# One block for the count matrix and the three graph layers, with relation rows fetched by POOL and stored by other engines

## The chip, the cores and the metric

The kernel runs on one core of one Trainium2 chip. The metric is the device time of one execution in microseconds (us); lower is better.

## The reference, cut to what matters

```python
def _L0_gnn_ref(x, edge_index, mask_embed, Wl, Wr, b, gamma, beta, rmean, rvar):
    N, E, D, L = (3125, 100000, 256, 3)
    src, dst = (edge_index[0], edge_index[1])
    h = x.at[0].set(mask_embed)
    deg = jax.ops.segment_sum(jnp.ones((src.shape[0],), h.dtype), dst, num_segments=N)
    deg = jnp.maximum(deg, 1.0)[:, None]
    for i in range(L):
        agg = jax.ops.segment_sum(h[src], dst, num_segments=N) / deg
        z = agg @ Wl[i] + b[i] + h @ Wr[i]
        z = (z - rmean[i]) * jax.lax.rsqrt(rvar[i] + EPS) * gamma[i] + beta[i]
        if i != L - 1:
            z = jax.nn.relu(z)
        z = z + h
        h = z
    return h
...
# in _L1_gnn_ref: a row of a 500-row relation table for every edge
    r_uv = r_hc[edge_type]
    m = clifford_linear(h_src * r_uv, msg_w, msg_b)
    gate = jax.nn.sigmoid(r_uv.reshape(r_uv.shape[0], -1) @ gate_w.T + gate_b)
...
x = x + _L0_gnn_ref(_layernorm(x), edge_index, ...)                # three layers, 103,125 edges
x = x + _L0_ffn_ref(_layernorm(x)[None], ...)[0]                   # 16 experts, top 2
x = x + _L1_gnn_ref(_layernorm(x), edge_index, edge_type_500, ...)  # relation messages
x = x + _L1_ffn_ref(_layernorm(x)[None], ...)[0]                   # 8 experts, top 2
```

Features have 256 columns. The part touched by the change is the first graph network: three times a sum of `h[src]` over the edges of each destination, divided by the degree, two 256 x 256 products, a normalization, relu and a residual. The second graph network needs, for each edge, a row of a table of 500 relations; those rows (260 floats with the gate) are fetched ahead of time, during the stages before it.

## The kernel before, in words

Nodes are held in NT = 25 tiles of 128. Edges are sorted by destination, 103,125 of them in 808 tiles of 128.

**Count matrix.** Since the same sum over edges is needed three times, `build_matrix` (L981) makes an fp8 matrix of 3200 x 3200 that counts the edges between a source and a destination. It works in 196 strips of SW = 16 destinations. A strip has DEEP = 5 tiles of edge records. DVE compares the source's place in its tile with a row of numbers (`b_at`, L1054, three of the five tiles; ACT makes the other two, L1085 and L1090) and writes five one-hot rows of 400 columns for the pair of source tile and destination (`b_oh`, L1058). PE multiplies them, five matmuls of 400 columns into one PSUM bank of a ring of seven (L1071), and ACT writes the bank into the matrix (L1095). Seven strips are a batch, there are 28 batches. For each batch SP reads seven starts from a table (L1026) and issues seven record DMAs (L1033); two batches are in flight (Q = 2). The loops are hardware loops of 14 strips.

**Layers.** `gnn0_layers` (L1113) then runs 3 x 25 destination tiles. h is held as three bf16 parts whose sum is h (256 columns each, with a column of ones for the degree). For each of 25 source tiles PE does one 512-column matmul (`ly_low`, L1181) and one of 256 or 257 (`ly_high`, L1182) with the same weights, a 128 x 128 block of the matrix. Between the sources it places the transposes (L1192) and the product with the two weight matrices (`ly_dense`, L1203) of the tile before. DVE adds the three sums, each divided by the degree, to z, the part of the layer computed ahead (`ly_zin`, L1257 to L1259), applies relu and adds h (L1261, L1264), and splits the next layer's features (L1272 to L1283). ACT copies (L1232, L1234, L1236) and makes one pass over a row block of the matrix for each tile of layers 0 and 1, a row sum (L1239) and the check that no count is above 15 (L1241). SP loads z (L1148) and stores the next layer's z (L1153). h itself stays in SBUF.

**Relation rows.** `RelationRows` (L1354) runs on POOL alone, beside every stage: cast a group of indices (L1375), gather a tile of 128 rows by an indirect DMA (L1383), and store a pair of tiles (L1390) from a ring of four. The 808 tiles are shared among the stages: 32 and 32 in `edge_blocks` (L360) and `gnn0_start` (L854), 160 in the matrix stage (buffer `rr_buf`), 408 in the layers (`rl_buf`), 176 in the first expert stage, by `RelationPairs` (L1618, `f_rr_buf`). A block of the program ends on all engines together.

Of the kernel before, what the change touches and what calls it, by code (L numbers as in the profile page):

```python
# [7 lines left out]
ALU = mybir.AluOpType  # L8
# [3 lines left out]
BF16 = mybir.dt.bfloat16  # L12
# [57 lines left out]
SHARES = (32, 32, 160, 408, 176)  # L70
assert sum(SHARES) == EDGE_TILES
GW = 3 * D + 2
TURN, DENSE = 9, 14
MOST = 15
# [285 lines left out]
def edge_blocks(nc, c, loads, relation):  # L360
# [6 lines left out]
    with Core(nc) as k:  # L367
# [486 lines left out]
def gnn0_start(nc, c, I, x_dram, h_table, room, g, z, folded, relations):  # L854

    with Core(nc) as k:
# [10 lines left out]
        work = RelationRows(nc, c, k, "r0", *relations[1], 2)  # L867
        with nc.Block() as block:
# [94 lines left out]
            def _(sp):  # L963
                sp.wait_ge(s_norm, NT)
                sp.dma_start(h_table.rearrange("(t p) d -> p t d", p=P), h[:, :, :]).then_inc(s_saved, 16)
                sp.wait_ge(s_w, 4)
# [3 lines left out]
                for b in range(NJ):  # L970
                    sp.wait_ge(s_z0, (b + 1) * J)
                    sp.dma_start(z[b * J * P:(b + 1) * J * P, :].rearrange("(t p) d -> p t d", p=P), f.z[:, b * J:(b + 1) * J, :])\
                        .then_inc(s_saved, 16)
                sp.wait_ge(s_saved, 16 * (5 + NJ))

            @block.gpsimd
            def _(pool):
                work(pool)


def build_matrix(nc, c, records, m, relation_work):  # L981

    with Core(nc) as k:
        Q, R, OWN, BANKS = 2, BATCH_S, DEEP - 2, 7
        unroll = Q * R
# [8 lines left out]
        pad = MW - STRIPS * SW  # L998
# [16 lines left out]

        strips = k.ps("b_strips", [P, BANKS, 512])
        s_rec = [k.sem(f"b_rec{q}") for q in range(Q)]
        s_code, s_gap, s_oh, s_at, s_sum, s_m = (k.sem(f"b_{x}") for x in ("code", "gap", "onehot", "at", "sum", "m"))
        rounds = STRIPS // unroll
        with nc.Block() as block:  # L1020

            @block.sync
            def _(sp):
                with sp.Fori(0, rounds) as i:
                    for q in range(Q):
                        starts = [sp.value_load(c.tab["a_start"][0:1, bass.ds(i * unroll + (q * R + n), 1)], min_val=0,  # L1026
                                                max_val=EDGE_TILES * P) for n in range(R)]

                        sp.wait_ge(s_oh, i * unroll + (q + 1) * R)
                        sp.wait_ge(s_at, i * unroll + (q + 1) * R)  # L1030
                        for n in range(R):
# [1379 lines left out]
```

## Time and profile before

| | us |
|---|---|
| median of 3 runs | 3740.11 (3734.98 to 3756.62) |
| profiled execution | 3740.51 |
| its span | 3738.8 |
| busy PE, DVE, ACT, POOL in the span | 2537.3, 1447.2, 1412.6, 2258.4 |

The span is the time from the first to the last instruction of that execution; busy times are averages over stages with different limits, so they are read stage by stage. The matrix stage lies from 272 to 661 us, the layers from 661 to about 1378, the first expert stage lies between 1380 and 2100, and the aggregation over relation edges follows. The granted TensorE clock, averaged over the run, is 0.832 of full speed.

### The profile page before, as it was taken

The page shows a single profiled execution, that of the slowest core. Times are in us where ns is not written, and L with a number is a line of the kernel's source. Part 1 is how long each engine was busy: PE and PEld are TensorE (multiplying, and loading weights), DVE is VectorE, ACT ScalarE, POOL GpSimd, SP SyncE. Part 2 cuts the span into 40 slices and gives each one's busy share as a digit, 9 for nine tenths or more (in the row PEclk, how much of TensorE's full clock was granted, in tenths as well). Part 3 has the DMA queues.
Part 4 walks back from the last instruction along what each step waited for, and adds up shares of the span by engine and source line. Part 5 has one row for each costly group of instructions (what it writes and reads, how often), then busy time and mean ns, then how long its engine had stood idle before and what let it go on. Part 6 is the DMA issues. An engine that isn't in the chain of part 4 may idle for free. (4 is left out here: it accounts for less than half of the span.)

```text
span 3738.8 us, 50034 instructions
## 1 busy us (share of the span) xinstructions
PE 2537.3 (68%) x12155; PEld 1728.3 (46%) x12155; DVE 1447.2 (39%) x4219; ACT 1412.6 (38%) x3615; POOL 2258.4 (60%) x2388
## 2 busy tenths in 40 slices
PE   0155564999999974977404666666666666699990
PEld 0122221555555544776403444444444445588990
DVE  4069997233333224000294444444444445200003
ACT  0037886334432002322105444444444443355550
POOL 0458888777777835777537777777777770111105
PEclk9998999999999985998756767676667667799995
DMA  2554343556666534668427777777777761442213
GB/s 104 185 179 129 115 115 112 177 186 194 193 193 192 184 99 163 194 211 264 150 66 229 207 204 206 200 206 206 205 202 204 201 187 53 148 136 79 81 29 106
DMA packets 320233, 606.95 MB, mean 162 GB/s; under 512 B 83139, under 2 KB 167817, under 8 KB 319239
## 3 DMA queue, kind: packets, MB, share of 16 engines
q0 software_dynamic: 123600, 359.43, 32.1%
q1 hardware_dynamic: 193591, 244.38, 21.1%
q8 instruction: 92, 1.51, 0.2%
q10 hardware_dynamic: 2848, 0.79, 0.1%
q14 instruction: 102, 0.84, 0.1%
HBM read 448.39 MB, written 157.66 MB: 162 GB/s over the span
## 5 line engine op out<-in xcount | busy, mean ns | idle before, releaser
L602 POOL DMA_INDIRECT agg_r_rows<-h_table,b_src x856 | 857.9, 1002 | 321.7 <-issue 217.6
L651 PE MATMUL agg_r_sums<-agg_r_rows,agg_r_onehot 128*128 128x257 f32 x1712 | 701.2, 558 | 380.9 <-DVE agg_r_rows L623 318.2
L651 PEld LDWEIGHTS agg_r_sums<-agg_r_rows,agg_r_onehot 128*128 128x128 f32 x1712 | 429.6, 274 | 636.9 <-issue 572.0
L1181 PE MATMUL ly_low<-parts,matrix 128*128 128x512 bf16 x1875 | 623.3, 380 | 29.1 <-PEq L112 29.1
L623 DVE TENSOR_TENSOR agg_r_rows<-agg_r_rows,agg_r_rel 128x514 f32<-128x514 f32 x428 | 299.0, 699 | 642.6 <-DMA agg_r_rows<-h_table,b_src 640.5
L1182 PE MATMUL ly_high<-parts,matrix 128*128 128x256 bf16 (+1 forms) x1875 | 513.0, 274 | 0.0
L1383 POOL DMA_INDIRECT rl_buf<-r_table,rl_kind x408 | 394.9, 968 | 153.6 <-issue 118.0
L569 ACT ACTIVATE agg_r_gap<-iota,b_near 128x128 f32<-128x128 f32 x856 | 295.0, 392 | 498.8 <-PE agg_r_sums L651 467.4
L1972 POOL DMA_INDIRECT f_xb<-xn_table,f_token x120 | 115.1, 960 | 502.1 <-PE f_pX L1780 363.0
L1790 PE MATMUL f_pH<-f_xT,f_w 128*128 128x128 f32 x2816 | 364.2, 289 | 67.3 <-DMA f_w<-in_L_ffn_w 44.9
L1790 PEld LDWEIGHTS f_pH<-f_xT,f_w 128*128 128x128 f32 x2816 | 349.4, 203 | 98.7 <-DMA f_w<-in_L_ffn_w 49.7
L1955 DVE TENSOR_TENSOR f_yb<-f_pY,f_b 128x256 f32<-128x256 f32 x120 | 50.9, 424 | 754.4 <-PE f_pY L1803 754.4
L1803 PE MATMUL f_pY<-f_w,f_hT 128*128 128x256 f32 x1408 | 331.4, 386 | 0.1
L1862 ACT ACTIVATE f_hT<-f_pH,f_b 128x128 f32<-128x128 f32 x704 | 197.7, 372 | 340.3 <-PE f_pH L1790 339.9
L1071 PE MATMUL b_strips<-b_oh,b_at 128*128 128x400 bf16 x980 | 206.6, 343 | 160.4 <-DVE b_oh L1058 125.7
L1181 PEld LDWEIGHTS ly_low<-parts,matrix 128*128 128x128 fp8e4 x1875 | 183.8, 98 | 254.9 <-issue 43.6
L1803 PEld LDWEIGHTS f_pY<-f_w,f_hT 128*128 128x128 f32 x1408 | 264.5, 195 | 32.6 <-DMA f_w<-in_L_ffn_w 0.4
L1383 POOL DMA_INDIRECT rr_buf<-r_table,rr_kind x160 | 251.0, 1569 | 46.6 <-issue 45.1
L1058 DVE TENSOR_SCALAR b_oh<-b_numbers,b_code 128x400 bf16<-128x400 f16 x980 | 250.8, 320 | 0.0
L1071 PEld LDWEIGHTS b_strips<-b_oh,b_at 128*128 128x128 bf16 x980 | 83.8, 98 | 283.6 <-ACT b_at L1090 166.8
L1651 POOL DMA_INDIRECT f_rr_buf<-r_table,f_rr_kind x176 | 174.7, 993 | 60.1 <-issue 50.6
L1182 PEld LDWEIGHTS ly_high<-parts,matrix 128*128 128x128 fp8e4 x1875 | 182.7, 97 | 42.0 <-issue 16.6
(373 smaller groups left out, 3076.3 us busy)
## 6 DMA issues: line engine op xcount, KB each, us to landing
agg_r_rel<-relation_rows SPq DMA_DIRECT2D x428, 260.0 KB, 3.2
relation_rows<-rl_buf POOLq DMA_DIRECT2D x204, 260.0 KB, 2.7
f_w<-in_L_ffn_W SPq DMA_DIRECT2D x28, 1024.0 KB, 5.7
relation_rows<-f_rr_buf POOLq DMA_DIRECT2D x88, 260.0 KB, 3.0
relation_rows<-rr_buf POOLq DMA_DIRECT2D x80, 260.0 KB, 2.7
f_w<-in_L_ffn_w SPq DMA_DIRECT2D x38, 512.0 KB, 6.1
f_ys<-f_yb SPq DMA_DIRECT2D x120, 128.0 KB
agg_r_rows<-h_table,b_src POOLq DMA_INDIRECT x856, 3.4
```

Of the source, the lines that this page charges most:

```text
L569: last = nc.scalar.activation(gap[:, n % BANKS, t, :], c.iota[:, 0:P], ACT.Abs, bias=c.tab["b_near"][:, bass.ds(g * 2 + t, 1)])
L602: pool.indirect_dma_start(rows[:, n % SLOTS, t, :], None, table, bass.IndirectOffsetOnAxis(ap=indices[:, t:t + 1], axis=0)).then_inc(s_row ...
L623: v.tensor_tensor(here, here, rel[:, n % SLOTS, :, 0:used], ALU.mult).then_inc(s_ready, 1)
L651: last = nc.tensor.matmul(sums[:, n % BANKS, 0:used], onehot[:, n % BANKS, t, :], rows[:, n % SLOTS, t, 0:used], start=t == 0, stop=t == 1)
L1058: last = v.tensor_scalar(oh[:, s, t, :], numbers[:, :], code[:, q, 1, n, t:t + 1], None, ALU.is_equal)
L1071: last = nc.tensor.matmul(strips[:, n % BANKS, 0:CODES], at[:, n % 2, t, :], oh[:, n % 2, t, :], start=t == 0, stop=t == DEEP - 1)
L1181: nc.tensor.matmul(low[:, n % 2, :], m[:, s, own], of[:, s, 0:2 * D], start=s == 0, stop=s == NT - 1)
L1182: last = nc.tensor.matmul(high[:, n % 2, 0:D + (l == 0)], m[:, s, own], of[:, s, 2 * D:3 * D + (l == 0)], start=s == 0, stop=s == NT - 1)
L1383: pool.indirect_dma_start(self.buf[:, n, g, :], None, self.table, bass.IndirectOffsetOnAxis(ap=self.kind[:, parity, at:at + 1], axis=0)).t ...
L1790: last = nc.tensor.matmul(pH[s][:, f * P:(f + 1) * P], w1b[:, s, h, f * P:(f + 1) * P], xT[:, s, h, :], start=h == 0, stop=h == KD - 1)
L1803: last = nc.tensor.matmul(pY[s][:, 0:D], hT[:, s, f, :], w2b[:, s, f, :], start=f == 0, stop=f == FC - 1)
L1862: nc.scalar.activation(hT[:, s, f, :], pH[s][:, f * P:(f + 1) * P], act_fn, bias=b1s[:, bass.ds(e, 1), f]).then_inc(s_hT, 1)
```

## The change

The matrix and the layers become one function, `matrix_and_layers`, in one block with unrolled loops. A step is one strip; from step 10 (AFTER) on, eight steps (PER) also carry one tile of layer 0, about three sources each. The strips keep three PSUM banks in place of seven. For each source of a tile PE now does three matmuls of 256 (257) columns into one accumulator in place of 512 and 257 columns into two, so DVE has one sum to add in place of three. SP reads records four batches ahead (Q = 4). In layer 1 ACT makes both passes over the matrix for a tile, in layer 0 none.

h no longer stays in SBUF: it travels with z in DRAM rows of 512 columns (`zh`), stored and loaded for each tile. The second set of parts and x share one SBUF region. `gnn0_start` stores h once more, beside z.

POOL only fetches relation rows, by indices that lie in SBUF as 32-bit integers, with no cast. They are stored by ACT in `edge_blocks`, by SP in `gnn0_start` and in the new block: five pairs per batch from batch 4 on, then four per tile, in layer 2 three. The shares are 40, 40, 608 and 120 tiles. In the expert stage POOL stores as before.

```diff
-SHARES = (32, 32, 160, 408, 176)
+SHARES = (40, 40, 608, 120)
...
 TURN, DENSE = 9, 14
+AFTER, PER = 10, P // SW
...
-        work = RelationRows(nc, c, k, "re", *relation, 2)
+        work = RelationRows(nc, c, k, "re", *relation)
         with nc.Block() as block:
             @block.gpsimd
             def _(pool):
-                work(pool)
+                work.fetch(pool, 0, work.pairs)
+            @block.scalar
+            def _(act):
+                work.store(act, 0, work.pairs)
+                work.stored(act)
             @block.sync
...
+                work.store(sp, 0, 8)
                 sp.wait_ge(s_norm, NT)
                 sp.dma_start(h_table.rearrange("(t p) d -> p t d", p=P), h[:, :, :]).then_inc(s_saved, 16)
+                sp.dma_start(z[:, D:2 * D].rearrange("(t p) d -> p t d", p=P), h[:, :, :]).then_inc(s_saved, 16)
...
+                    work.store(sp, 8 + 2 * b, 10 + 2 * b)
                     sp.wait_ge(s_z0, (b + 1) * J)
-                    sp.dma_start(z[b * J * P:(b + 1) * J * P, :].rearrange("(t p) d -> p t d", p=P), f.z[:, b * J:(b + 1) * J, :])\
+                    sp.dma_start(z[b * J * P:(b + 1) * J * P, 0:D].rearrange("(t p) d -> p t d", p=P), f.z[:, b * J:(b + 1) * J, :])\
                         .then_inc(s_saved, 16)
-                sp.wait_ge(s_saved, 16 * (5 + NJ))
+                sp.wait_ge(s_saved, 16 * (6 + NJ))
+                work.store(sp, 8 + 2 * NJ, work.pairs)
+                work.stored(sp)
...
+    strip_of = [min(PER * (d + 1), STRIPS) for d in range(NT)]
+    steps = AFTER + PER * NT
+    pieces = [slice(NT * q // PER, NT * (q + 1) // PER) for q in range(PER)]
...
-        Q, R, OWN, BANKS = 2, BATCH_S, DEEP - 2, 7
...
+        Q, R, OWN, BANKS = 4, BATCH_S, DEEP - 2, 3
...
+                def records_in(b):
+                    starts = [sp.value_load(c.tab["a_start"][0:1, b * R + n:b * R + n + 1], min_val=0, max_val=EDGE_TILES * P) for n in range(R)]
+                    if b >= Q:
+                        sp.wait_ge(s_oh, (b - Q + 1) * R)
+                        sp.wait_ge(s_at, (b - Q + 1) * R)
+                    for n in range(R):
+                        src = records[bass.ds(starts[n], DEEP * P), :].rearrange("(p k) c -> p k c", p=P)
+                        sp.dma_start(rec[:, b % Q, n, :, :], src).then_inc(s_rec[b % Q], 16)
...
-                    sp.dma_start(zin[:, n % 2, :], z_dram[l][d * P:(d + 1) * P, :]).then_inc(s_zin[n % 2], 16)
+                    if l < 2:
+                        sp.dma_start(zin[:, n % 2, :], zh[l][rows, :]).then_inc(s_zin[n % 2], 16)
+                    else:
+                        sp.dma_start(zin[:, n % 2, 0:D], zh[l][rows, 0:D]).then_inc(s_zin[n % 2], 16)
+                        sp.dma_start(zin[:, n % 2, D:2 * D], x_dram[rows, :]).then_inc(s_zin[n % 2], 16)
...
-                for n in range(2 * NT):
+                stored = done = 0
+                for b in range(BATCHES_S):
+                    records_in(b)
+                    while done < NT - 2 and PER * done + AFTER + 2 * PER <= (b - Q + 1) * R:
+                        tile_out(done)
+                        tile_in(done + 2)
+                        done += 1
+                    if b >= Q:
+                        work.store(sp, stored, stored + work.RING + 1)
+                        stored += work.RING + 1
+                for n in range(done, 2 * NT):
                     tile_out(n)
                     tile_in(n + 2)
...
+                    upto = min(stored + work.RING, work.pairs)
+                    work.store(sp, stored, upto)
+                    stored = upto
                 for n in range(2 * NT, 3 * NT - 2):
                     tile_in(n + 2)
+                    upto = min(stored + work.RING - 1, work.pairs)
+                    work.store(sp, stored, upto)
+                    stored = upto
+                work.store(sp, stored, work.pairs)
+                work.stored(sp)
...
-                        nc.tensor.matmul(low[:, n % 2, :], m[:, s, own], of[:, s, 0:2 * D], start=s == 0, stop=s == NT - 1)
-                        last = nc.tensor.matmul(high[:, n % 2, 0:D + (l == 0)], m[:, s, own], of[:, s, 2 * D:3 * D + (l == 0)],
-                                                start=s == 0, stop=s == NT - 1)
+                        nc.tensor.matmul(acc[:, n % 2, 0:D + one], m[:, s, own], of[:, s, 2 * D:3 * D + one], start=s == 0, stop=False)
+                        nc.tensor.matmul(acc[:, n % 2, 0:D], m[:, s, own], of[:, s, 0:D], start=False, stop=False)
+                        last = nc.tensor.matmul(acc[:, n % 2, 0:D], m[:, s, own], of[:, s, D:2 * D], start=False, stop=s == NT - 1)
...
+                for n in range(steps):
+                    if n < STRIPS:
+                        strip(n)
+                    if n < AFTER:
+                        continue
+                    d, q = divmod(n - AFTER, PER)
+                    if q == 0:
+                        free(d)
+                        pe.wait_ge(s_m, strip_of[d])
+                    last = add(d, range(NT)[pieces[q]])
+                    if q == PER - 1:
+                        last.then_inc(s_sum, 1)
+                    if d and q == 3:
+                        turn(d - 1)
+                    if d and q == 5:
+                        ahead(d - 1)
...
+                for n in range(steps + PER):
+                    if n < STRIPS:
+                        places(n)
+                    if 0 < n <= STRIPS:
+                        keep(n - 1)
+                    for late, piece in ((AFTER + 4, turned), (AFTER + 6, high), (AFTER + 8, middle)):
+                        d, q = divmod(n - late, PER)
+                        if q == 0 and 0 < d < NT:
+                            piece(d - 1)
...
+                    turned(n)
+                    high(n)
+                    middle(n)
+                    d = n - NT
+                    if d >= 0:
                         nc.scalar.activation(junk[:, :], m[:, d, :], ACT.Copy, accum_out=c.deg[:, 0, d:d + 1], saturate=False).then_inc(s_count, 1)
-                    else:
-                        nc.scalar.activation(junk[:, :], m[:, d, :], ACT.Relu, bias=minus[:, 0:1], accum_out=above[:, d:d + 1], saturate=False).then_inc(s_count, 1)
-                    act.wait_ge(s_count, n + 1)
+                        act.wait_ge(s_count, 2 * d + 1)
+                        nc.scalar.activation(junk[:, :], m[:, d, :], ACT.Relu, bias=minus[:, 0:1], accum_out=above[:, d:d + 1], saturate=False)\
+                            .then_inc(s_count, 1)
...
-                    dve.wait_ge(s_zin[n % 2], 16 * (n // 2 + 1))
+                    dve.wait_ge(s_zin[n % 2], zin_count(n))
                     st.link(v.scalar_tensor_tensor(z, a[:, 0:D], r, z, ALU.mult, ALU.add))
-                    st.link(v.scalar_tensor_tensor(z, a[:, D:2 * D], r, z, ALU.mult, ALU.add))
-                    st.link(v.scalar_tensor_tensor(z, b[:, 0:D], r, z, ALU.mult, ALU.add))
                     if l < 2:
-                        v.scalar_tensor_tensor(h[:, d, :], z, 0.0, h[:, d, :], ALU.max, ALU.add).then_inc(s_new, 1)
+                        if n >= 2:
+                            dve.wait_ge(s_out[n % 2], 16 * (n // 2))
+                        v.scalar_tensor_tensor(out[:, n % 2, D:2 * D], z, 0.0, own, ALU.max, ALU.add).then_inc(s_new, 1)
                     else:
-                        dve.wait_ge(s_x[d // J], 16)
-                        v.tensor_tensor(h[:, d, :], z, h[:, d, :], ALU.add).then_inc(s_new, 1)
+                        v.tensor_tensor(x1[:, d, :], z, own, ALU.add).then_inc(s_new, 1)
...
+                for n in range(steps + PER):
+                    if n < STRIPS:
+                        onehots(n)
+                    d, q = divmod(n - AFTER - PER, PER)
+                    if q == 0 and 0 < d < NT:
+                        if d == 1:
+                            dve.wait_ge(s_fold, 16)
+                        split(d - 1)
+                    if q == 2 and 0 <= d < NT:
+                        if d:
+                            lowest(d - 1)
+                        finish(d)
+                for n in range(NT, 2 * NT + 1):
+                    if n - 1 == NT:
+                        dve.wait_ge(s_fold, 32)
                     split(n - 1)
+                    lowest(n - 1)
                     finish(n)
...
+    RING = 4
...
+    def fetch(self, pool, first, upto):
+        for q in range(first, upto):
+            n = q % self.RING
+            if q >= self.RING:
+                pool.wait_ge(self.s_out[n], 16 * (q // self.RING))
+            pool.sem_inc(self.s_gate, 1)
+            for g in range(2):
+                at = self.first + 2 * q + g
                 pool.indirect_dma_start(self.buf[:, n, g, :], None, self.table,
-                                        bass.IndirectOffsetOnAxis(ap=self.kind[:, parity, at:at + 1], axis=0)).then_inc(self.s_row[n], 16)
-        def store(h, n):
-            pool.wait_ge(self.s_row[n], h * (16 * size) + 16 * size)
+                                        bass.IndirectOffsetOnAxis(ap=self.c.kinds[:, at:at + 1], axis=0)).then_inc(self.s_row[n], 16)
+    def store(self, engine, first, upto):
+        for q in range(first, upto):
+            n, at = q % self.RING, self.first + 2 * q
+            engine.wait_ge(self.s_row[n], 32 * (q // self.RING + 1))
+            engine.dma_start(self.out[:, at:at + 2, :], self.buf[:, n, :, :]).then_inc(self.s_out[n], 16)
...
-                    work.kinds(pool)
                     while asked < BEFORE:
-                        work.pair(pool, asked)
+                        work.both(pool, asked)
                         asked += 1
...
-        c.kinds = c.sb("kinds", [P, EDGE_TILES], I16)
+        c.kinds = c.sb("kinds", [P, EDGE_TILES], I32)
...
+        shared = c.sb("parts1_and_x", [P, NT * GW // 2])
+        c.x = shared[:, 0:NT * D].rearrange("p (t d) -> p t d", d=D)
+        gb = shared[:, :].bitcast(BF16).rearrange("p (t w) -> p t w", t=NT)
+        x1, h_tables = gnn0(nc, c, I, edges, r_table, relation_rows, gb)
```

How the instructions stand on SP in the matrix stage before, at the end of one batch and the beginning of the next:

```order
L1033 DMA b_rec<-records 128x20
L1033 ISA
L1033 DMA b_rec<-records 128x20
L1026 ISA
L1026 TENSOR_LOAD a_start
L1026 ISA x3
L1026 TENSOR_LOAD a_start
```

And now, at the end of a batch from the fourth on (`rl_row0` to `rl_row3` are the arrivals in the ring of relation rows):

```order
L1060 DMA b_rec<-records 128x20
L1081 DMA zh<-ly_out 128x512 [waits ly_z0]
L1073 DMA ly_zin<-zh 128x512 [waits ly_new]
L1423 DMA relation_rows<-rl_buf 128x520 [waits rl_row3]
L1423 DMA relation_rows<-rl_buf 128x520 [waits rl_row0]
L1423 DMA relation_rows<-rl_buf 128x520 [waits rl_row1]
L1423 DMA relation_rows<-rl_buf 128x520 [waits rl_row2]
L1423 DMA relation_rows<-rl_buf 128x520 [waits rl_row3]
L1053 TENSOR_LOAD a_start
L1053 ISA x2
```

Between the last record DMA of a batch and the first start of the next stand now a tile's store and load and five stores of relation rows, of which the first and the fifth use the same slot of the ring.

On PE before, a strip of the matrix stage:

```order
L1071 MATMUL b_strips<-b_oh,b_at 128x400 [waits b_onehot,b_at]
L1071 MATMUL b_strips<-b_oh,b_at 128x400 x4
```

And now a strip of the woven block with its three sources of a layer-0 tile:

```order
L1123 MATMUL b_strips<-b_oh,b_at 128x400 [waits b_onehot,b_at,b_m]
L1123 MATMUL b_strips<-b_oh,b_at 128x400 x4
L1134 MATMUL ly_acc<-parts,matrix 128x257
L1135 MATMUL ly_acc<-parts,matrix 128x256
L1136 MATMUL ly_acc<-parts,matrix 128x256
L1134 MATMUL ly_acc<-parts,matrix 128x257
L1135 MATMUL ly_acc<-parts,matrix 128x256
L1136 MATMUL ly_acc<-parts,matrix 128x256
```

The layer's matmuls came after all strips and now stand between two of them, behind the strip's waits.

## Rows read from the trace of the kernel before

**Rows 1.** Windows view. Columns: stretch, us, busy PE, PEld, DVE, ACT, POOL, PEclk, DMA, GB/s
```profile
272.00:661.00 389.00, 206.56 (x980) 83.79 (x980) 342.91 (x1628) 292.42 (x784) 331.60 (x261) 0.92 0.40 115
661.00:914.00 253.00, 252.74 (x1383) 143.24 (x1384) 82.51 (x241) 94.18 (x119) 196.63 (x248) 0.99 0.60 186
```

**Rows 2.** Timeline, 499.5 to 501.2. Columns: start, us, engine, line, operation
```profile
499.52 0.57 DVE L1054 TENSOR_SCALAR b_at<-b_iota,b_rec 128x128 bf16<-128x128 bf16 x3
499.75 1.01 PE L1071 MATMUL b_strips<-b_oh,b_at 128*128 128x400 bf16 x5 [1.03 <-DVE b_oh L1058]
...
500.29 2.78 POOL L1383 DMA_INDIRECT rr_buf<-r_table,rr_kind  x1 [0.30 <-issue]
...
501.17 0.57 DVE L1054 TENSOR_SCALAR b_at<-b_iota,b_rec 128x128 bf16<-128x128 bf16 x3
```

**Rows 3.** Tile b_rec. Columns: line, count: shortest/median/longest ns, first and last start
```profile
L1033 SPq MOVE b_rec<-records x196: 29/29/38, 280.8 to 610.1; - x196
L1045 DVE TENSOR_TENSOR b_code<-b_rec,b_strip_ids x28: 194/203/216, 286.4 to 618.8; 128x35 f32<-128x35 f32 x28
```

**Rows 4.** Timeline of PE, first row after the matrix stage
```profile
661.26 0.58 PE L1181 MATMUL ly_low<-parts,matrix 128*128 128x512 bf16 x1 [29.07 <-PEq L112]
```

**Rows 5.** Timeline of PE in a layer-0 tile
```profile
666.57 0.27 PE L1182 MATMUL ly_high<-parts,matrix 128*128 128x257 bf16 x1
666.68 0.38 PE L1181 MATMUL ly_low<-parts,matrix 128*128 128x512 bf16 x1
666.90 0.27 PE L1182 MATMUL ly_high<-parts,matrix 128*128 128x257 bf16 x1
```

**Rows 6.** Timeline of SP in the layers
```profile
913.73 0.32 SPq L1153 DMA_DIRECT2D z<-ly_out  x1
914.15 0.41 SPq L1148 DMA_DIRECT2D ly_zin<-z  x1
923.88 0.32 SPq L1153 DMA_DIRECT2D z<-ly_out  x1
```

**Rows 7.** Tile ly_zin in the layers
```profile
L1257 DVE SCALAR_TENSOR_TENSOR ly_zin<-ly_low,rdeg,ly_zin x75: 482/483/486, 672.6 to 1376.4; 128x256 f32<-128x256 f32 x75
...
L1264 DVE TENSOR_TENSOR x<-ly_zin,x x25: 424/425/426, 1181.2 to 1377.9; 128x256 f32<-128x256 f32 x25
```

**Rows 8.** Waits, 1380 to 2100: waiting, waited for, us in total, times, longest
```profile
PE f_pX L1780 <- DMA f_xb<-xn_table,f_token: 32.0, 12, 12.7
```

**Rows 9.** Timeline of SP in the start stage
```profile
227.93 38.89 SPq L972 DMA_DIRECT2D z<-matrix  x5
```

**Rows 10.** DMA issues, 276 to 661: count, KB each, us to landing
```profile
relation_rows<-rr_buf POOLq DMA_DIRECT2D x80, 260.0 KB, 2.7
...
rr_buf<-r_table,rr_kind POOLq DMA_INDIRECT x160, 2.9
```

**Rows 11.** Line 1026, SP's register loads
```profile
L1026 SPq TENSOR_LOAD <-a_start x196: 262/267/572, 275.9 to 602.7; - x196
```

**Rows 12.** Timeline of SP, one batch of records
```profile
485.33 3.52 SPq L1033 DMA_DIRECT2D b_rec<-records  x7
```

**Rows 13.** The page's costliest groups, POOL; then tile rl_buf
```profile
L1383 POOL DMA_INDIRECT rl_buf<-r_table,rl_kind x408 | 394.9, 968 | 153.6 <-issue 118.0
...
L1383 POOL DMA_INDIRECT rr_buf<-r_table,rr_kind x160 | 251.0, 1569 | 46.6 <-issue 45.1
...
L1390 POOL DMA_DIRECT2D relation_rows<-rl_buf x204: 544/588/615, 669.6 to 1345.4; - x102
```

**Rows 14.** Timeline of ACT in layer 1
```profile
954.28 2.95 ACT L1241 ACTIVATE ly_junk<-matrix,ly_minus 128x3200 fp8e4<-128x3200 fp8e4 x1
...
959.90 0.38 ACT L1232 ACTIVATE ly_hT<-ly_turns 128x256 f32<-128x256 f32 x1 [2.59 <-issue]
```

**Rows 15.** Windows view, two more stretches
```profile
580.00:620.00 40.00, 23.76 (x119) 9.77 (x117) 39.86 (x194) 34.97 (x94) 36.34 (x22) 1.00 0.33 93
2100.00:2500.00 400.00, 266.45 (x678) 167.57 (x677) 165.92 (x328) 170.12 (x471) 306.74 (x306) 0.70 0.73 204
```

More of the change, by code:

```diff
@@ L997, in build_matrix @@
         iota_low = k.sb("b_iota", [P, P], BF16)
-        pad = MW - STRIPS * SW
+        g = [ga, gb]
+        fold = k.sb("ly_fold", [P, 5 * D])
+        zin, out = k.sb("ly_zin", [P, 2, 2 * D]), k.sb("ly_out", [P, 2, 2 * D])
+        hT = k.sb("ly_hT", [P, 2, KD, P])
+        rest = k.sb("ly_rest", [P, D])
+        above, clip = k.sb("ly_above", [P, NT]), k.sb("ly_clip", [P, 1])
+        minus, over, wide = k.sb("ly_minus", [P, 1]), k.sb("ly_over", [P, 1]), k.sb("ly_wide", [1, 1])
+        work = RelationRows(nc, c, k, "rl", *relation)
         with Core(nc) as kk:
@@ L1113, in gnn0_layers @@
-def gnn0_layers(nc, c, m, ga, z_dram, folded, x_dram, relation):
-    h = c.x
-    with Core(nc) as k:
-        g = [ga, k.sb("parts1", [P, NT, GW], BF16)]
-        fold = k.sb("ly_fold", [P, 5 * D])
-        zin, out = k.sb("ly_zin", [P, 2, D]), k.sb("ly_out", [P, 2, D])
-        hT = k.sb("ly_hT", [P, 2, KD, P])
-        rest = k.sb("ly_rest", [P, D])
-        junk = k.sb("ly_junk", [P, MW], F8)
-        above, clip = k.sb("ly_above", [P, NT]), k.sb("ly_clip", [P, 1])
-        minus, over, wide = k.sb("ly_minus", [P, 1]), k.sb("ly_over", [P, 1]), k.sb("ly_wide", [1, 1])
-        low, high = k.ps("ly_low", [P, 2, 512]), k.ps("ly_high", [P, 2, 512])
-        turns, dense = k.ps("ly_turns", [P, 2, 512]), k.ps("ly_dense", [P, 2, 512])
+        s_code, s_gap, s_oh, s_at, s_strip, s_m = (k.sem(f"b_{x}") for x in ("code", "gap", "onehot", "at", "strip", "m"))
@@ L1304, in _ @@
             def _(pool):
-                work(pool)
+                work.fetch(pool, 0, work.pairs)
 def relation_tables(nc, c, I, r_table):
@@ L1421, in gnn0, with __init__ @@
-def gnn0(nc, c, I, edges, r_table, relation_rows):
+    RING = 4
+    def __init__(self, nc, c, k, name, r_table, out, first, tiles, alone=False):
+        self.c, self.table, self.first, self.pairs = c, r_table, first, tiles // 2
+        assert tiles % 2 == 0 and self.pairs >= self.RING
+        self.out = out[0:EDGE_TILES * P, :].rearrange("(p k) c -> p k c", p=P)
+        self.buf = k.sb(f"{name}_buf", [P, self.RING, 2, W1])
+        self.s_row = [c.pool_sem(f"{name}_row{s}") for s in range(self.RING)]
+        self.s_out = [c.pool_sem(f"{name}_out{s}") if alone else k.sem(f"{name}_out{s}") for s in range(self.RING)]
+        self.s_gate = k.sem(f"{name}_gate")
@@ L1702, in feed_forward @@
         token_f, token = k.sb(f"{name}_token_f", [P, tiles]), k.sb(f"{name}_token", [P, tiles], I32)
[L1703 removed]
+        work = RelationRows(nc, c, k, f"{name}_rr", *relation, True) if relation else None
         w1b = k.sb(f"{name}_w1", [P, 2, KD, nf])
@@ L1976, in _ @@
                         while asked < upto:
-                            work.pair(pool, asked)
+                            work.both(pool, asked)
                             asked += 1
                 if work:
-                    work.rest(pool)
+                    work.store(pool, work.pairs - 2, work.pairs)
+                    work.stored(pool)
 class RowNorm:
```

307 lines of the change are left out of this document (96 added, 211 removed).

## The prediction

> **What bounds the kernel now.** I read the program in stages (the windows view), then in each stage the waits, then the order of time inside one batch and one tile. One execution has a span of 3738.8 us and took 3740.5 us; the runs shown have a median of 3740.1, so the sum below needs no shift.
>
> The change sits between 276 and 1378 us. In the matrix stage (272 to 661) DVE is busy 343 of 389 us, PE 207 [rows 1]; inside a strip PE waits about 1.0 us for DVE's one-hot rows, and DVE starts a strip every 1.65 us (499.52, 501.17) [rows 2]. 196 strips at that pace are 323 us; from DVE's first strip at 286.4 [rows 3] to the end of the strips at about 632 it takes 346. Then PE stands still for 29.1 us, until the next block opens at 661 [rows 4]: POOL is still at its relation rows. The layers are PE-bound: PE is busy in all 253 us of the window [rows 1]. A source is one 512-column and one 256-column matmul; they start 0.22 and 0.11 us apart [rows 5]. A tile takes 10.16 us (tile stores at 913.73 and 923.88) [rows 6]: 25 x 0.33 = 8.23, two transposes 0.22, four dense matmuls 1.72. In the third layer it is (1377.9 - 1181.2) / 24 = 8.20 us [rows 7]. In the first expert stage PE waits 32.0 us for token rows that POOL fetches [rows 8].
>
> **Start stages.** Shares 32 to 40 each: 4 more pairs of tiles, but stores leave POOL's queue. One 3.2 MB store of h is added and two relation stores stand behind the last wait on SP. The issues of the five z stores stretch over 38.9 us, tied to DVE's tiles [rows 9], so most of the DMA fits beside them. Bounds 0 and +15; I take +5, near the price of one store (2.7 us to landing [rows 10]) and its issue twice.
>
> **The woven block, PE.** Eight steps carry eight strips and one layer-0 tile. Strip: five matmuls of 400 columns are over in 1.01 us, the last of them in flight for 0.34, so they start 0.168 us apart and a strip takes 5 x 0.168 = 0.84 [rows 2]; x 8 = 6.7. Tile: three 256-column matmuls per source. The trace has such a matmul with a weight load in front start 0.11 us before the next one (666.57, 666.68) [rows 5]; 75 x 0.1115 = 8.36, plus 0.22 and 1.72 = 10.3. Together 17.0 us per eight strips, 2.13 per strip.
>
> What speaks against is that each source now has three weight loads. The Trainium skill (TensorE: Matmul & The Clock Gate, The mechanism) says a load overlaps with matmuls only for another row group, and its LDWEIGHTS section gives columns / 1.2 ns; by that the third load would cost about 107 ns, some 200 us over 1875 sources. By the trace the load costs nothing there.
>
> **DVE.** Eight strips 8 x 1.65 = 13.2, the code pair 0.4 per seven strips, slowing by POOL as before (mean period 346 / 196 = 1.76) makes 14.1. The tile: in the layers DVE is busy 82.5 us in 253, which is 24.9 tiles, so 3.3 us each; two of the three 0.483 us multiply-adds go, 2.35 stay, with links 2.7 [rows 1, 7]. Sum 16.8. PE and DVE are equal and two strips apart at most, so I take 2.2 us per strip for the pair of them, 15.4 per batch of seven.
>
> **SP, the new chain.** SP now reads starts, issues records, moves tiles and stores relation rows. From batch 4 on it stores five pairs per batch through a ring of four: the fifth waits for the slot of the first. Its loop per batch, none of it hidden:
> - seven starts 4.2 us (275.9 to 280.8 is 4.9 for the first seven, with the loop's register work besides) [rows 3, 11], seven record issues 3.5 [rows 12];
> - tile store and load 0.32 + 0.41 [rows 6], in 7 of 8 batches: 0.7;
> - first store to landing 2.7 [rows 10]; POOL is then released: 0.3, a gather 1.25, 0.3, second gather to landing 2.9 [rows 10], fifth store's issue 0.35.
>
> Sum 16.2 us. A gather is 0.97 us beside the layers and 1.57 beside the one-hots [rows 13]; DVE has gaps in the woven block, so 1.25. POOL by itself needs 5 x (2 x 1.25 + 0.6) = 15.5. With both near equal I take 16.5 us, over the 15.4 of PE and DVE. Ends: 15.4 and 18.7 (POOL with 1.57).
>
> The time from SP's first load (275.9, now 280.9): fold and first tiles 1.3, four batches without stores 4 x 7.7 = 30.8; batch 27 begins at 32.1 + 23 x 16.5 = 411.6. In it tile 19's input is issued (8.1) and lands (2.7): 422.4. DVE needs that input behind strip 172. A tile's input is issued only some ten strips ahead of its use, so this binds long before the four batches of records run out. The other 24 strips x 2.2 = 52.8, the last 14 pieces and two dense parts of PE 18.5: 493.7.
>
> **Layers 1 and 2.** 25 x 10.29 + 25 x 8.34 = 465.8, and 1.0 for the last tile. If the 256-column pace were 0.117 instead, +27 us: the upper end of that term. Hidden beside PE:
> - ACT now makes both passes over the matrix in layer 1. Today the pass starts at 954.28 and ACT is next needed at 959.90 [rows 14]; the second adds 3.2, so ACT is free about 0.8 us late, but the dense part comes 1.4 us after the transposes. It is hidden with 0.3 us to spare.
> - POOL owes four pairs per tile: 8 x (0.97 + 0.3) = 10.2 us against 10.29. SP sees a tile's input 9 us early, so a small lag is carried.
> - The wider tile traffic: DMA share 0.60 in the layers [rows 1].
>
> **After the block.** 28 pairs fewer in the expert stage. Of the 32.0 us of waits for token rows 12.7 is the longest, ahead of the first tile [rows 8], which stays (POOL is busy with 12 pairs there, as before); of 19.3 I take 12 (bounds 0 and 20), since weight loads wait beside them.
>
> **Sum.** The block ends at 280.9 + 493.7 + 465.8 + 1.0 = 1241.4 instead of 1378.3: -136.9, the +5 inside. Experts -12. 3740.5 - 148.9 = 3591.6, I say 3592.
>
> **Rivals.**
> - *SP's chain does not bind*: four stores of five meet no wait and gathers are at 0.97. PE and DVE set 15.4 per batch: 23 x 1.1 = 25 us less: 3567. For it: SP had free time in the old stage. Against: the ring is one short of the five stores.
> - *POOL binds*: gathers stay at 1.57, since DVE's one-hots run back to back as in 580 to 620, where POOL got only 22 instructions in 40 us [rows 15]. A batch is 18.7: 23 x 2.2 = +51: 3643. One gather among the one-hots took 2.78 us [rows 2]. The Trainium skill (SBUF — State Buffer, Terms) says of the port pair that DVE and GpSimd share that the loser is blocked for the other's whole instruction; by that a gather would lose 0.32 us at a time, and the trace shows more, 2.78 against 0.97 us, where the instructions stand back to back.
> - *The third weight load shows*: 0.107 us x 1250 = 134 in layers 1 and 2, and 67 in the woven block, of which 25 is under SP's chain: +176, to 3768. Against it stands the 0.11 us between starts [rows 5].
> - *Slower: PE's clock drops in the woven block.* PE now works in bursts with waits. In the later aggregation the granted clock is 0.70 with PE busy 266 of 400 us [rows 15]. At the lower level (1.2 GHz) a tile with its strips costs PE 34 us instead of 17 against 18.9 of the SP chain: +15 us per tile, 25 tiles +377: 3969. It decides from some ten tiles at that level (149 / 15). Against: in 580 to 620 the clock is 1.00 with PE busy 24 of 40 us, less than in the woven block.
> - *The change moves nothing*: POOL sets the block's length with 304 pairs at the present 3.33 us ((1345.4 - 669.6) / 203) [rows 13] are 1012 us instead of 961, +51: 3643. POOL loses its stores (0.59 us each), which speaks against.
>
> **How the numbers follow.** Forecast 0.50, chain not binding 0.15, POOL binds in either form 0.25, third weight load 0.02, lower clock 0.04, and 0.04 for losses that I don't see and that eat the gain. Range: below, 25 us of the chain, 8 of the experts and 5 of the start give 3554, and some more if the coupling is looser: 3540. Above, POOL at 3643, the 27 us of PE's pace and the 12 of the experts: 3682, so 3685. A change of this kernel under 0.5% (19 us) cannot be told from none. Faster 0.90 (the first three), slower 0.06 (weight load and clock), same 0.04.
>
> **What the profile would show.** PE without the 29 us hole; DVE's wait for ly_zin in the woven block about 1.3 us per tile (18.9 against 15.4 x 8/7 = 17.6); SP's record issues 16.5 us apart from batch 5 on; POOL waiting for the slot of the batch's first store; gathers of 1.25 us; 256-column matmuls 0.11 us apart; layer tiles at 10.3 and 8.3 us; the last layer tile ending near 1241. Wrong it is if tiles in layer 1 take 11 us or more, if the clock column falls below 0.9 there, or if SP's batches are as long as PE's own work.

## The result and the profile after

The changed kernel takes 3632.26 us (median of 4 runs, 3613.96 to 3639.46) where the kernel before takes 3739.12 (4 runs). The ratio is 0.9698, 95% interval 0.9657 to 0.9738: 3.0% faster, 107 us. Forecast were 3592, with a range of 3540 to 3685. The profiled execution has a span of 3634.2 us, 104.6 less than before.

The windows view of the changed kernel, by the stages of the new block; the columns are those of [rows 1]:

```profile
330.00:700.00 370.00, 308.95 (x2114) 214.36 (x2112) 286.19 (x1296) 219.97 (x610) 220.75 (x201) 0.94 0.59 172
...
818.00:1075.00 257.00, 253.77 (x2017) 203.21 (x2015) 59.77 (x149) 167.98 (x168) 183.28 (x193) 1.00 0.82 254
1075.00:1284.00 209.00, 207.33 (x1881) 182.16 (x1879) 25.52 (x61) 10.47 (x11) 123.71 (x131) 1.00 0.68 205
```

In the woven part (330 to 700) no engine is full: PE 309 of 370 us, DVE 286, POOL 221. In layers 1 and 2 PE is busy throughout, as it was [rows 1]. What moved, from the first and last matmuls of each stage in the two profiled executions:

| us | before | after | difference |
|---|---|---|---|
| first strip begins | 288.7 | 290.3 | +1.6 |
| first strip to the last layer matmul | 1087.6 | 991.9 | -95.7 |
| from there to the first aggregation matmul | 615.0 | 603.9 | -11.1 |
| from there to the end of the span | 1747.5 | 1748.1 | +0.6 |

The last strip ends at 797.3, layer 1 begins at 816.5, the last layer matmul ends at 1282.2. So layer 0, which took 25 tiles of 10.2 us behind the matrix stage and a hole, is now over 184 us after the time at which the strips alone ended before (632.2), and the 29 us hole [rows 4] is gone.

The timeline of SP in one batch of the changed kernel (a row joins instructions of one kind; the second number is the stretch they cover), then POOL's in the same stretch:

```profile
585.90 3.47 SPq L1060 DMA_DIRECT2D b_rec<-records  x7
589.42 0.43 SPq L1081 DMA_DIRECT2D zh<-ly_out  x1
589.90 0.47 SPq L1073 DMA_DIRECT2D ly_zin<-zh  x1
590.42 10.64 SPq L1423 DMA_DIRECT2D relation_rows<-rl_buf  x5
```

```profile
594.61 1.32 POOL L1415 DMA_INDIRECT rl_buf<-r_table,kinds  x1 [5.84 <-DMA relation_rows<-rl_buf]
596.24 2.01 POOL L1415 DMA_INDIRECT rl_buf<-r_table,kinds  x1 [0.30 <-issue]
```

The first store goes out at 590.42. POOL stands idle for 5.84 us until that store has landed, gathers the next pair from 594.61 on, and only then does SP's fifth store go, which closes the 10.64 us. In that time SP issues nothing else, and the next tile's input waits behind it. This is the chain that the prediction drew.

The same in the waits of the woven block (330 to 830: who waited for what, us in total, times, longest):

```profile
POOL rl_buf L1415 <- DMA relation_rows<-rl_buf: 123.9, 42, 6.5
...
PE b_strips L1123 <- DVE b_oh L1272: 81.8, 19, 19.6
...
DVE ly_zin L1284 <- DMA ly_zin<-zh: 63.7, 10, 18.7
```

PE waits for DVE's one-hots, DVE for the tile's input, the input for SP's place in line, and SP for POOL's pair. No wait of the three names SP itself. SP's own waits, in 309 to 730, do name POOL's gathers, and next to nothing else (0.6 us for a tile's output):

```profile
SPq L1423 <- DMA rl_buf<-r_table,kinds: 164.6, 40, 8.3
```

DVE's 63.7 us are not spread over the tiles: 58 of them are four waits of 8.2, 16.0, 15.1 and 18.7 us, each behind a batch in which SP moves no tile (6, 10, 18 and 26). Around each of them PE has little to do, and the granted clock falls to its lower level, 0.50 or 1.2 GHz, for example here:

```profile
586.00:600.00 14.00, 4.08 (x17) 2.63 (x18) 6.33 (x28) 0.50 (x1) 6.63 (x7) 0.50 0.59 173
```

Two matmul rows of layer 1 of the changed kernel, as an answer to [rows 5]: start and length.

```profile
900.05 0.27 PE L1136 MATMUL ly_acc<-parts_and_x,matrix 128*128 128x256 bf16 x1
900.16 0.27 PE L1134 MATMUL ly_acc<-parts_and_x,matrix 128*128 128x256 bf16 x1
```

They start 0.11 us apart although each has its own weight load.

### The profile page after: what moved, and what is told of

It is laid out like the page before. It is cut to its first block and busy times, and to the rows that moved or that the text cites. A ratio compares the mean times of both kernels' runs of the same rounds, so it can differ in the third digit from the quotient of the medians.

```text
span 3634.2 us, 51269 instructions
## 1 busy us (share of the span) xinstructions
PE 2513.8 (69%) x14030; PEld 1920.2 (53%) x14030; DVE 1374.4 (38%) x4069; ACT 1404.1 (39%) x3615; POOL 1946.2 (54%) x1964
## 5 line engine op out<-in xcount | busy, mean ns | idle before, releaser
L608 POOL DMA_INDIRECT agg_r_rows<-h_table,parts_and_x x856 | 861.5, 1006 | 322.7 <-issue 213.8
L1415 POOL DMA_INDIRECT rl_buf<-r_table,kinds x608 | 616.3, 1014 | 349.2 <-DMA relation_rows<-rl_buf 186.1
L575 ACT ACTIVATE agg_r_gap<-iota,parts_and_x 128x128 f32<-128x128 f32 x856 | 295.1, 392 | 492.7 <-PE agg_r_sums L657 461.0
L1136 PE MATMUL ly_acc<-parts,matrix 128*128 128x256 bf16 x1250 | 343.7, 275 | 0.0
L1134 PE MATMUL ly_acc<-parts,matrix 128*128 128x257 bf16 (+1 forms) x1250 | 342.1, 274 | 0.0
L1135 PE MATMUL ly_acc<-parts,matrix 128*128 128x256 bf16 x1250 | 342.1, 274 | 0.0
L1415 POOL DMA_INDIRECT f_rr_buf<-r_table,kinds x120 | 120.8, 1007 | 137.8 <-POOLq L113 99.9
L1123 PEld LDWEIGHTS b_strips<-b_oh,b_at 128*128 128x128 bf16 x980 | 94.9, 99 | 188.3 <-issue 109.4
L623 DVE TENSOR_TENSOR acc<-acc,agg_r_sums 128x257 f32 (+1 forms) x431 | 179.1, 415 | 13.6 <-PE agg_r_sums L657 13.5
L578 ACT ACTIVATE agg_r_onehot<-agg_r_gap 128x256 f32<-128x256 f32 x428 | 178.2, 416 | 13.5
```

What stands on the lines that cost most here:

```text
L575: last = nc.scalar.activation(gap[:, n % BANKS, t, :], c.iota[:, 0:P], ACT.Abs, bias=c.tab["b_near"][:, bass.ds(g * 2 + t, 1)])
L608: pool.indirect_dma_start(rows[:, n % SLOTS, t, :], None, table, bass.IndirectOffsetOnAxis(ap=indices[:, t:t + 1], axis=0)).then_inc(s_row ...
L1123: last = nc.tensor.matmul(strips[:, n % BANKS, 0:CODES], at[:, n % 2, t, :], oh[:, n % 2, t, :], start=t == 0, stop=t == DEEP - 1)
L1134: nc.tensor.matmul(acc[:, n % 2, 0:D + one], m[:, s, own], of[:, s, 2 * D:3 * D + one], start=s == 0, stop=False)
L1135: nc.tensor.matmul(acc[:, n % 2, 0:D], m[:, s, own], of[:, s, 0:D], start=False, stop=False)
L1136: last = nc.tensor.matmul(acc[:, n % 2, 0:D], m[:, s, own], of[:, s, D:2 * D], start=False, stop=s == NT - 1)
```

## The experiments

Ratios are to the kernel before, run beside each. The first four experiments ran on another chip than the rest: there the kernel before took 3905.67 us. They stand first, since they misled at first, and the last section comes back to them.

**Five slots in the ring, first chip**, one edit in the changed kernel (the ring was a constant of the class):

```diff
-        work = RelationRows(nc, c, k, "rl", *relation)
+        work = RelationRows(nc, c, k, "rl", *relation, ring=5)
```

> The changed kernel with one edit: the ring of relation rows in the woven block has five slots in place of four, with the same five stores per batch. Theory A (SP's own chain sets the batch: the fifth store waits for the landing of the first and for two gathers, 18.3 us per batch of seven strips in the changed kernel): the wait goes, a batch falls to PE's and DVE's own pace of 15.4 to 16 us, 23 batches give 50 to 65 us, 3570 to 3580 us in all. Theory B (PE and DVE in each other's waits set 18.3, and SP's wait is slack): no change, 3632. Theory C (POOL's gathers set it): no change either, and POOL without idle time in the woven block.

Measured: 4090.95 us, ratio 1.048 (1.042 to 1.055). No theory had a slower kernel in it.

**Four stores per batch, first chip:**

```diff
-SHARES = (40, 40, 608, 120)
+SHARES = (40, 40, 560, 168)
...
-                        work.store(sp, stored, stored + work.RING + 1)
-                        stored += work.RING + 1
+                        work.store(sp, stored, stored + 4)
+                        stored += 4
```

> The changed kernel with four stores per batch in place of five, ring of four, and shares 40, 40, 560, 168: the 24 pairs go to the first expert stage. Theory A: no store of a batch waits for a slot of the same batch, a batch falls to 15.4 to 16 us, -50 to -65, and the expert stage takes back up to 10: 3575 to 3590 us. Theory B: the woven block stays, 3632 to 3640. Theory C (POOL): a batch falls by one pair of 2.8 us, to 15.5, as by theory A; the ring of five tells A and C apart.

Measured: 4059.89 us, ratio 1.041 (1.036 to 1.046). Both traces show waits that the changed kernel's trace does not have: between 330 and 830 us DVE's `b_at` stands 132 us (27 times) in the first and 77 us (18 times) in the second with nothing of this core named that it waits for.

**No relation stores before layer 1, first chip:**

```diff
-                        work.store(sp, stored, stored + work.RING + 1)
-                        stored += work.RING + 1
+                        pass
...
-                    upto = min(stored + work.RING, work.pairs)
+                    upto = min(stored + work.RING, work.pairs) if n >= NT else 0
```

> The changed kernel with no relation stores before layer 1 (the rows are all made, those left over in a tail behind the last layer, some 135 pairs, about 380 us, so the total says nothing). It measures the woven block without SP's and POOL's relation work. Theory A: PE and DVE at 15.4 to 16 us per batch of seven strips, the block's strips over by about 740 in place of 797. Theory B: 18 us per batch as before.

The single run took 4254.8 us, with the tail of leftover rows in it. The strips ran from 301.3 to 728.7 us. SP began batch 7 at 344.9 and batch 27 at 653.4: 15.4 us per batch, to the tenth what theory A gives PE and DVE. The strips themselves, from strip 10 to the last, go at 17.6 us per eight, which is the same pace. The window of 340 to 700 of this kernel, columns as before:

```profile
340.00:700.00 360.00, 345.70 (x2448) 243.16 (x2448) 323.29 (x1502) 254.17 (x705) 0.00 (x0) 1.00 0.14 35
```

PE is busy 346 of 360 us, at full clock, and DVE 323. With no relation work the woven block is PE's, with DVE close behind.

**The kernel before with other shares only, first chip:**

```diff
-SHARES = (32, 32, 160, 408, 176)
+SHARES = (32, 32, 128, 416, 200)
```

> The kernel before with shares 32, 32, 128, 416, 200 only: POOL gets 32 tiles less in the matrix stage, 8 more in the layers and 24 more in the first expert stage. What part of the 107 us was PE's 29 us of standing still at the end of the matrix stage, which needs no weaving? If that hole is POOL's alone, it shrinks to under 5 us and the time is 3739 - 25 + up to 10 in the expert stage: 3715 to 3725 us. Rival: the strips themselves run slower or the expert stage takes it all back: 3739.

Measured: 3890.54 us, ratio 0.996 (0.994 to 0.998), 15 us less. PE's layers begin at 632.5, 2 us behind the strips: the hole is gone.

**The changed kernel unaltered**, as a base for what follows, on a chip where the kernel before took 3742.46:

> The changed kernel itself, unaltered, on the chip of the experiments, since the kernel before took 3906 us there and not 3739. Theory A' (the slower batches of the ring of five and of four stores come from that chip or its memory, not from their edit): the changed kernel is slow there too, ratio to before above 1.03. Theory D (five or four stores issued back to back slow every engine, and the ring of four held them apart): the ratio stays at 0.97 and the two edits cost 7 to 8 per cent.

Measured: 3631.89 us, ratio 0.971 (0.966 to 0.977). The changed kernel was not run on the first chip, so what its own ratio is there stays open.

**Five slots again, beside it:**

> The ring of five slots again, beside the unaltered changed kernel. Theory A: 50 to 65 us below the changed kernel of the same chip. Theory D: some 300 us above it, as the first run's ratios (1.048 against 0.970) would have it. Theory B: equal.

Measured: 3577.32 us, ratio 0.957 (0.952 to 0.963), 55 us less than the changed kernel, inside theory A's 50 to 65. The strips end at 744.1 in place of 799.8. SP's batches 4 to 26 take 16.0 us on average in place of 18.3. SP gets ahead of the strips in the first of these batches; the strips, from strip 10 to the last, go at 18.8 us per eight in place of 21.1.

**Four stores again:**

> Four stores per batch with shares 40, 40, 560, 168 again, beside the unaltered changed kernel. Theory A: 40 to 60 us below it. Theory D: some 270 us above. Theory B: equal, or up to 10 us above for the expert stage.

Measured: 3562.16 us, ratio 0.952 (0.947 to 0.957), 70 us less, 10 more than theory A allowed. The strips end at 727.6. SP's batches 4 to 26 take 15.0 us on average, the strips 18.0 us per eight, which is 15.7 per seven. Its window of 340 to 700:

```profile
340.00:700.00 360.00, 338.66 (x2403) 237.97 (x2401) 325.88 (x1477) 250.52 (x696) 212.57 (x194) 1.00 0.60 178
```

The clock stands at 1.00, and PE is busy 339 us, where the unaltered kernel shows 0.93 and 292 (the last run of it, below).

**Two of the five stores ahead of the records**, ring of four, shares untouched:

```diff
-                def records_in(b):
+                def records_in(b, early):
...
+                    work.store(sp, early, early + 2 if b >= Q else early)
                     for n in range(R):
...
-                        work.store(sp, stored, stored + work.RING + 1)
+                        work.store(sp, stored + 2, stored + work.RING + 1)
```

> The changed kernel with two of a batch's five stores placed between the starts and the record DMAs, and three behind the tile's store and load; ring of four as it is. Theory A: the fifth store's slot was released some 5 us earlier, SP's chain is down to about 14 us, a batch to PE's and DVE's 15.4 to 16, -50 to -60 us against the changed kernel. Theory B: equal. Theory D: between, since two and three stores stand together in place of four.

Measured: 3568.39 us, ratio 0.954 (0.949 to 0.959), 63.5 us less, a little more than the 50 to 60 expected, the strips over at 738.6, 15.6 us per batch of SP and 18.5 us per eight strips. The number of stores, the ring, the gathers and the bytes are those of the changed kernel: only the order on SP differs. That rules out POOL's capacity as the bound, and theory D.

**Four stores per batch, but not woven:**

```diff
-AFTER, PER = 10, P // SW
+AFTER, PER = 196, P // SW
```

> The version of four stores per batch (shares 40, 40, 560, 168) with only the weaving undone: the first tile of layer 0 starts after step 196 in place of step 10, all else as it is. What is weaving itself worth? PE's work per strip and per tile stays, 0.84 and 10.3 us; the strips alone go at DVE's 1.76 us. If weaving hides one of the two stages behind the other: strips 345 us and layer 0 258 us one after the other, layer 1 starts at about 895 in place of 747, +147 us: about 3710, near the kernel before less its hole. Rival (most of the gain comes from the fetch without casts, the wait-free stores and the smaller DVE part of a tile, not from weaving): under +60 us, 3620 or less.

Measured: 3758.54 us, ratio 1.003 (1.000 to 1.006): 196 us above the woven version (194 above the version with every wait taken off SP, below, which ran beside it), more than the 147 expected. Layer 1 begins at 924.6 in place of 746.8, 178 of the 196. Layer 0 behind the strips is as expected, the strips are not: 381 us, not 345. Its waits from 300 to 700:

```profile
PE b_strips L1123 <- DVE b_oh L1272: 79.8, 57, 7.5
...
PE b_strips L1123 <- ACT matrix L1211: 74.2, 113, 1.2
...
DVE b_code L1261 <- DMA b_rec<-records: 33.1, 16, 6.2
```

DVE runs out of records 16 times. Strips alone need a batch every 12 us from SP, and SP with four stores needed 10 to 21. PE also waits 74 us for the bank that ACT has yet to empty, one of three where there were seven. So 36 of the 196 us (381 less 345) are strips that ran slower than expected, beside these two waits, and not layer 0 without its overlap; an unwoven version that keeps seven banks and spreads the stores was not run.

**Other shares of the kernel before, again**, with the kernel before at 3750.66:

> The kernel before with shares 32, 32, 128, 416, 200 only, again, since the first run was on a chip where the kernel before took 3906 us. There PE's hole of 29 us was gone and the ratio 0.996. On a chip with 3740 the theory of the hole gives -29 for the hole and up to +12 for 12 more pairs in the expert stage: 3710 to 3725.

Measured: 3738.99 us, ratio 0.997 (0.996 to 0.998), 12 us less, and not the 3710 to 3725 expected. The hole is gone: the layers begin at 631.5 in place of 661.3 and end at 1345.8 in place of 1376.3. But the stretch from there to the aggregation is 640.7 us in place of 615.0. PE's wait for token rows in it, before and in this kernel, is 32.0 [rows 8] and

```profile
PE f_pX L1780 <- DMA f_xb<-xn_table,f_token: 43.5, 17, 12.1
```

So twelve more pairs in the expert stage took back most of the hole; of the 26 us the wait explains 11.5, the other 14 I can't place.

**The changed kernel unaltered, once more,** with the kernel before at 3750.66, as a base for the unwoven version above and the next one:

> The changed kernel unaltered, as the base of this call. On a chip like the last one 3632, ratio 0.970. On a chip like the first (kernel before at 3906): theory A' expects a ratio above 1.03, theory D 0.97.

Measured: 3631.62 us, ratio 0.968 (0.966 to 0.971). Its window of 340 to 700:

```profile
340.00:700.00 360.00, 292.03 (x2008) 203.02 (x2006) 273.91 (x1236) 209.09 (x580) 209.59 (x194) 0.93 0.58 171
```

**Every wait taken off SP:** four stores, two of them early, ring of five, shares 40, 40, 560, 168.

> A version meant to take every wait off SP: four stores per batch, ring of five slots, two stores ahead of the record DMAs, shares 40, 40, 560, 168. Four stores alone came to 15.0 us per batch, and PE's own work is 7/8 x 17.0 = 14.9. If PE is the bound there, nothing is left: 3562, equal to four stores. If SP's order still costs, 3545 or less.

Measured: 3564.76 us, ratio 0.950 (0.948 to 0.952): equal to four stores alone (3562.16, beside another base). The strips end at 725.9, against 727.6, and go at 17.9 us per eight. Once the fifth store is out of the way, taking more waits off SP gains nothing. PE is busy 340 and DVE 328 of the 360 us from 340 to 700: what is left is the two of them. The best version, four stores per batch, is 2% under the changed kernel and 5% under the kernel before.

## Why the prediction was right

**What bounded the kernel.** Right. The hole went, the layers were PE-bound before and after. The version without weaving shows that overlapping strips with layer 0 carries the gain: with the new fetching, sums, orders and three banks but without it the kernel is no faster than before. It is not a clean measure of the overlap, since three banks cost the strips time that weaving hides.

**PE and DVE in the woven block.** Right, both in PE's work of 17.0 us per eight strips and in the 17.6 (15.4 per batch) that the prediction took for PE and DVE together. Without relation work the strips went at 17.6, with four stores per batch at 18.0, and there PE is busy 339 of 360 us, about 17 of each 18.0. SP's mean of 15.0 us per batch in that version must not be set beside PE's 14.9: SP works ahead of the strips there, and its first batches are short.

**SP's chain of 16.5 us per batch.** The mechanism was right, and three edits that take away that wait, each in another way, gained 55, 63 and 70 us; the edit of the order alone gained 63. The size was off: batches 4 to 26 took 18.3 us. Over batches 5 to 26 of the trace the mean of each term is, against its forecast:

| us | forecast | measured |
|---|---|---|
| starts | 4.2 | 4.4 |
| records and tile | 4.2 | 4.4 |
| first store to POOL's gather | 3.0 | 4.6 |
| first to second gather | 1.55 | 1.4 |
| second gather to the fifth store | 2.9 | 3.2 |
| its issue | 0.35 | 0.4 |
| sum | 16.2 | 18.4 |

The term that was too small is the 2.7 us from store to landing, taken from POOL's stores, one per pair and none behind a tile's transfers [rows 10]. Here it goes out right behind a tile's 256 KB store and load, with three more of its own kind behind it. In the five of these batches that have no tile (5, 6, 10, 18, 26) the gather starts 3.1 to 3.6 us after the store, in the others 4.2 to 6.0. That points at the tile's two transfers; no run took them away alone. The page of DMA issues of the changed kernel, 340 to 750, has the median at

```profile
relation_rows<-rl_buf SPq DMA_DIRECT2D x111, 260.0 KB, 3.7
```

23 batches by 1.8 us are 41, and layer 1 began 42 us later than forecast (816.5 against 774.6). That is all of the 40 us between 3592 and 3632: the block's other terms were off by 4 us at most (SP's first load 2 us early, the four batches without stores 1.5 us short, the part behind the beginning of batch 27 4 us long) and nearly cancel.

**POOL.** A gather took 1.10 us on average in the woven block (224 of them, 18 over 1.5 us), not 1.25 and far from 1.57. The weaving helps POOL, but the gaps of DVE that the prediction argued with do not explain it alone: between 340 and 620 us a gather takes 1.09 us on average with four stores per batch, 1.43 in the unwoven version and 1.69 in the kernel before, while DVE is busy 90%, 87% and 99% of the time. The rival "POOL binds" gave 3643, closer to the 3632 measured than the forecast is, but by luck: POOL waited 124 us for stores to land, and an order of stores that leaves its work as it is gained 63 us.

**DVE's wait for a tile's input.** Forecast were 1.3 us per tile. It is 63.7 us between 330 and 830, about 2.7 per tile, which goes with a batch of 18.4 us in place of 16.5; and it comes in lumps behind the batches without a tile, which was not foreseen.

**Layers 1 and 2, 466 us.** Measured 465.7. The third weight load costs nothing that shows: 0.11 us between starts. The rule of the Trainium skill (TensorE: Matmul & The Clock Gate, The mechanism) that the prediction weighed against the row, a load overlapping only for another row group, would by its estimate have made the kernel 176 us longer, 134 of them in these two layers; the trace does not agree with it. The same section also has the engine pull a load ahead into a background weight buffer, and with that the 0.11 us agree. ACT's second pass is hidden, without a gap: in layer 1 it goes from the second pass into the next tile's copy.

```profile
849.46 2.96 ACT L1247 ACTIVATE ly_junk<-matrix,ly_minus 128x3200 fp8e4<-128x3200 fp8e4 x1
...
852.55 0.38 ACT L1219 ACTIVATE ly_hT<-ly_turns 128x256 f32<-128x256 f32 x1
855.45 0.38 ACT L1223 ACTIVATE parts<-ly_dense 128x256 bf16<-128x256 f32 x1 [2.51 <-PE ly_dense L1156]
```

The wait of 2.51 us for the dense part is the slack that remains.

**The clock.** The rival of a whole block at the lower level did not come about, but a trace of it is there: 0.93 in the woven block with SP's waits, 1.00 with four stores per batch; before it was 0.92 in the matrix stage and 0.99 in the layers [rows 1]. The low stretches lie at DVE's long waits, and the six terms of SP's batch, which hold no wait for PE, add up to the whole batch without them.

**Start and experts.** +1.6 us against +5, and -11.1 against -12; the three profiled executions of the changed kernel have 599.8, 603.9 and 608.7 us in that stretch, so its last digits mean little.

**The range.** 3632 lies in it. The forecast itself was 40 us low, of a change of 107: the gain was over-stated by more than a third.

## What to carry to other kernels

When an in-order queue issues n items through a ring of fewer than n slots, the last issue waits for a full round trip of the first, and all that is queued behind it waits too: issue as many as the ring has, or put other work between. Take a transfer's time to landing from a place where as much is in flight as will be, not from one that went out alone. Weaving two stages paid here, where one was bound by DVE and the other by PE, and its worth is measured by undoing the order alone, with buffers that suit the unwoven order, not by comparing with the old kernel. Measure a pace on the engine that does the work: the queue that feeds it can run ahead, and its mean then looks too fast.

## What was not expected of the hardware

The first chip. The kernel before took 3906 us there and 3739 to 3751 elsewhere, but not evenly: with the other shares, of which there are traces on both chips, its layers took 715.6 us against 714.3, its aggregation 1222 against 1110. The ring of five, 3577 us on one chip, took 4091 on the other. The windows of its layer 1 on the first chip, and of layer 1 of the unaltered changed kernel on the second:

```profile
970.00:1330.00 360.00, 281.35 (x1947) 203.28 (x1944) 57.79 (x143) 164.31 (x164) 187.26 (x197) 0.90 0.59 182
```

```profile
830.00:1070.00 240.00, 238.85 (x1903) 191.80 (x1901) 56.02 (x139) 163.52 (x162) 173.00 (x182) 1.00 0.82 255
```

The whole layer took 378 us there (960.7 to 1339.1) and 256 on the second chip. In fortieths of that window the first chip moves 15 to 31 GB/s at times and 250 at others; ahead of such stretches PE starts single matmuls 1.4 us apart (997.9 to 1004.9). The old layers, which move 186 GB/s steadily, do not suffer, and the woven block without relation work (35 GB/s) goes at 17.6 us per eight strips; layer 1, which moves 255 on the second chip, does. Whether the memory, the DMA engines or the fetching of instructions stands still there, no run tells. It is left open, and with it whether the change is a gain on such a chip at all.
